# Output blocks copied out by ScalarE and added by GpSimd, with one buffer each for the high half and the e row

## What is computed

```
proj = layernorm(x) @ in_proj_w            # gate 4096, x 4096, B 128, C 128, dt 64
x, B, C = silu(causal_conv4(...))          # per channel
dt = softplus(dt + dt_bias); dA = -dt * exp(A_log); cum = cumsum(dA) per chunk
Y = (C B^T * decay * dt) x  +  C state * exp(cum)  +  D * x      # 64 heads of 64
hidden = Y * silu(gate)
out = (hidden * rsqrt(mean(hidden^2) + eps) * norm_w) @ out_proj_w
```

## Time and profile before

| | us |
|---|---|
| three runs | 1464.09, 1466.99, 1469.27; median 1466.99 |
| profiled execution | 1469.74 |
| its span, first to last instruction | 1468.0 |
| its busy time: PE / DVE / ACT / POOL | 1336.6 / 1190.8 / 1007.1 / 823.1 |

### The profile page before, as it was taken

One profiled execution on the slowest core, in us unless ns is written; L12 is line 12 of the kernel. 1 busy time (PEld: TensorE's weight loads), 2 busy tenths in 40 slices (PEclk: granted clock), 3 DMA queues, 4 the chain that ended last, 5 costly groups with the idle time before them and its releaser, 6 DMA issues. The chain is left out here.

```text
span 1468.0 us, 27111 instructions
## 1 busy us (share of the span) xinstructions
PE 1336.6 (91%) x8896; PEld 1137.1 (77%) x8896; DVE 1190.8 (81%) x2643; ACT 1007.1 (69%) x2067; POOL 823.1 (56%) x896
## 2 busy tenths in 40 slices
PE   5889887767999999999999999999999999986998
PEld 4778776556888888888888888888888888864887
DVE  5753443576999999999999999999999999986433
ACT  1114433667889988888988898888899888861332
POOL 1004211004678787877878787797787878681000
PEclk9999987978999999999999999999999999995999
DMA  6221000223454554454564645644435544324000
GB/s 128 66 87 36 15 15 0 65 65 76 121 111 98 118 125 114 119 112 98 119 125 115 118 101 114 116 123 121 113 101 109 129 113 117 96 73 186 15 14 29
DMA packets 102085, 136.43 MB, mean 93 GB/s; under 512 B 27744, under 2 KB 49856, under 8 KB 101824
## 3 DMA queue, kind: packets, MB, share of 16 engines
q1 hardware_dynamic: 99840, 132.67, 37.6%
q10 hardware_dynamic: 2112, 2.10, 0.4%
HBM read 124.76 MB, written 9.96 MB: 92 GB/s over the span
## 5 line engine op out<-in xcount | busy, mean ns | idle before, releaser
L845 ACT ACTIVATE M<-cum_row,cum_table 128x128 f32<-128x128 f32 x1024 | 312.2, 390 | 0.0
L1240 DVE SCALAR_TENSOR_TENSOR xs<-psum,conv_w_sb,xs 128x509 f32<-128x509 f32 (+2 forms) x384 | 284.2, 740 | 0.4
L985 POOL TENSOR_TENSOR hid_lo<-hid,hid_hi 128x512 fp32r<-128x512 f32 x128 | 191.2, 1494 | 65.4 <-PE psum L40 59.6
L1028 POOL TENSOR_TENSOR hid<-hid,sg 128x512 f32<-128x512 f32 x128 | 165.7, 1295 | 89.5 <-DVE hid L1308 89.4
L1017 POOL TENSOR_TENSOR squares<-squares,sq 128x512 f32<-128x512 f32 x124 | 160.2, 1292 | 75.2 <-ACT sq L822 75.2
L1267 DVE TENSOR_TENSOR M<-M,CB 128x1024 f32<-128x1024 f32 x128 | 182.9, 1429 | 0.0
L1623 PE MATMUL psum<-M,xdt 128*64 128x128 f32 x2048 | 140.1, 279 | 20.8 <-DVE psum L1299 20.8
L827 ACT ACTIVATE sg<-psum 128x512 f32<-128x512 f32 x128 | 75.2, 587 | 102.2 <-PE psum L40 94.6
L1623 PEld LDWEIGHTS psum<-M,xdt 128*64 128x64 f32 x2048 | 109.9, 136 | 43.2 <-DVE M L1267 25.0
L1600 PE MATMUL psum<-xend,B_tok 128*128 128x128 f32 x1024 | 140.3, 281 | 2.1 <-DVE carry L1291 1.9
L859 ACT ACTIVATE xs<-psum,conv_b_sb,conv_w_sb 128x512 f32<-128x512 f32 x128 | 98.7, 771 | 52.7 <-PE psum L40 52.7
(11 more groups left out here) (210 smaller groups left out, 3432.5 us busy)
## 6 DMA issues: line engine op xcount, KB each, us to landing
cum_row<-cum_scratch SPq DMA_DIRECT2D x256, 256.0 KB, 4.6
e_row<-e_scratch SPq DMA_DIRECT2D x256, 128.0 KB, 3.5
xw_raw<-L_attn_in_proj_w_dram SPq DMA_DIRECT2D x32, 128.0 KB, 5.1
wo_raw<-L_attn_out_proj_w_dram SPq DMA_DIRECT2D x32, 128.0 KB, 4.6
gw_raw<-L_attn_in_proj_w_dram SPq DMA_DIRECT2D x16, 256.0 KB, 5.8
x_res<-_attn_hidden_states_dram ACTq DMA_DIRECT2D x4, 512.0 KB, 9.3
x_scratch<-x_res SPq DMA_DIRECT2D x4, 512.0 KB, 2.6
x_res<-x_scratch SPq DMA_DIRECT2D x1, 2048.0 KB, 7.6
```

The source lines that it names most:

```text
L845: last = nc.scalar.activation(M[:, v % 3, h, c * CH:(c + 1) * CH], cum_row[:, v % 2, h, c * CH:(c + 1) * CH], ACT.Relu, bias=scalar_of(CUM ...
L985: nc.gpsimd.tensor_tensor(hid_lo[:], hid[:, v % 2, :], hid_hi[:, v % 2, :].bitcast(F32), ALU.subtract).then_inc(hid_lo_done, 1)
L1028: nc.gpsimd.tensor_tensor(hid[:, v % 2, :], hid[:, v % 2, :], sg[:, v % 8, :], ALU.mult).then_inc(hid_done, 1)
L1240: nc.vector.scalar_tensor_tensor(xs[:, v % 7, shift:], psum[:, X_BANK + v % 2, 0:TT - shift], tap_of(v, step), xs[:, v % 7, shift:], ALU.m ...
```

## The change

`add_out` goes from DVE. In its place ACT, in the slot after a block ends (a phase slot, behind `square`), copies the two PSUM banks out in `take_out`: in the first group straight into `mixed`, later into a new tile `part` with one buffer. POOL then adds the halves of `part` into `mixed` in `add_part`, two and three slots after that phase slot began, that is in the slots with s mod 4 = 2 and 3, behind `gate`, the squares and `split_hid`. `out_proj` of the next block now waits for the copies (`out_taken`), and the copies wait for both adds of the block before (`mixed_done`). `hid_hi` and `e_row` get one buffer each, with their waits one slot nearer. POOL does `gate` ahead of the squares, and in the slots with s mod 4 = 1 the squares come behind `split_hid`. In the phase slots `evac_g` applies silu itself, so one silu of four goes. X_SLOTS and G_SLOTS move ahead by up to a slot.

```diff
-    e_row = sb("e_row", [P, 2, TT], F32)
+    e_row = sb("e_row", [P, TT], F32)
-    hid_hi = sb("hid_hi", [P, 2, TT], F32R)
+    hid_hi = sb("hid_hi", [P, TT], F32R)
+    part = sb("part", [P, KT, TT], F32)
...
-    X_SLOTS = (5, 7, 8, 10)
-    G_SLOTS = (6, 9)
+    X_SLOTS = (5, 7, 7, 9)
+    G_SLOTS = (6, 8)
...
-                sp.wait_ge(off_scaled, nth(v - 2))
+                sp.wait_ge(off_scaled, nth(v - 1))
...
+            def take_out(v):
+
+                t = at_slot(v)[1]
+                act.wait_ge(out_done, nth(v))
+                if v == GP - 1:
+                    act.wait_ge(cum_out, 16 * 2 * NT)
+                if v >= SLOTS:
+                    act.wait_ge(mixed_done, KT * ((v - SLOTS) // GP))
+                for m in range(KT):
+                    to = mixed[:, m, tile(t)] if v < SLOTS else part[:, m, :]
+                    nc.scalar.activation(to, psum[:, OUT_BANK + m, :], ACT.Copy).then_inc(out_taken, 1)
...
             for s in range(-8, ALL):
                 if alive(s):
                     square(s)
+                if s > 0 and s % GP == 0:
+                    take_out(s - 1)
                 phase = s % GP == 0 and alive(s + 4)
                 if phase:
-                    for v in range(s + 4, s + 8):
+                    for v in range(s + 4 if s < 0 else s + 5, s + 8):
                         silu_g(v)
...
-                    evac_g(s + 8)
+                    evac_g(s + 8, ACT.Silu if phase else ACT.Copy)
...
-                pool.wait_ge(out_done, nth(v - 2))
+                pool.wait_ge(out_done, nth(v - 1))
...
+            def add_part(v, m):
+
+                t = at_slot(v)[1]
+                pool.wait_ge(out_taken, KT * (v // GP) + m + 1)
+                nc.gpsimd.tensor_tensor(mixed[:, m, tile(t)], mixed[:, m, tile(t)], part[:, m, :],
+                                        ALU.add).then_inc(mixed_done, 1)
...
             for s in range(-8, ALL):
-                if alive(s):
-                    add_squares(s)
+                after_silu = s % GP == 1
...
                 if alive(s + 1):
                     gate(s + 1)
+                if alive(s) and not after_silu:
+                    add_squares(s)
+                if alive(s + 1):
                     split_hid(s + 1)
+                if alive(s) and after_silu:
+                    add_squares(s)
                 g, u = divmod(s, SLOTS)
+                if s % GP in (2, 3) and SLOTS <= s - s % GP - 1:
+                    add_part(s - s % GP - 1, s % GP - 2)
...
+            for m in range(KT):
+                add_part(ALL - 1, m)
...
-            def add_out(v):
...
-                if s >= 0 and s % GP == GP - 1:
-                    add_out(s)
...
-                    pe.wait_ge(mixed_done, KT * (v // GP))
+                    pe.wait_ge(out_taken, KT * (v // GP))
```

More of the change, by code:

```diff
@@ L467, in macaron @@
     cum_in, xw_in, wo_in = [[sem(f"{n}{i}") for i in range(2)] for n in ("cum_in", "xw_in", "wo_in")]
-    e_in, gw_in = [sem(f"e_in{i}") for i in range(2)], sem("gw_in")
+    e_in, gw_in = sem("e_in"), sem("gw_in")
     halo_in, halo_step, halo_done = sem("halo_in"), sem("halo_step"), sem("halo_done")
-    folded = sem("folded")
+    folded, out_taken = sem("folded"), sem("out_taken")
     wo_hi_done, wo_lo_done, hid_hi_done, hid_lo_done = [sem(n) for n in ("wo_hi_done", "wo_lo_done", "hid_hi_done", "hid_lo_done")]
@@ L618, in load_e @@
                 head = 2 * pair_of(v)
-                sp.wait_ge(off_scaled, nth(v - 2))
+                sp.wait_ge(off_scaled, nth(v - 1))
                 for h in range(2):
-                    sp.dma_start(e_row[h * HP:(h + 1) * HP, v % 2, :],
+                    sp.dma_start(e_row[h * HP:(h + 1) * HP, :],
                                  e_dram[head + h:head + h + 1, tile(at_slot(v)[1])].partition_broadcast(HP)
-                                 .rearrange("p o t -> p (o t)")).then_inc(e_in[v % 2], 16)
+                                 .rearrange("p o t -> p (o t)")).then_inc(e_in, 16)
             for p in range(2):
@@ L822, in square, with evac_g @@
                 nc.scalar.activation(sq[:], hid[:, v % 2, :], ACT.Square).then_inc(sq_done, 1)
-            def evac_g(v):
+            def evac_g(v, how=ACT.Copy):
                 act.wait_ge(g_proj, nth(v))
                 act.wait_ge(hid_done, nth(v - 8))
-                nc.scalar.activation(sg[:, v % 8, :], bank(G_BANK), ACT.Copy).then_inc(g_evac, 1)
+                nc.scalar.activation(sg[:, v % 8, :], bank(G_BANK), how).then_inc(g_evac, 1)
             def silu_g(v):
@@ L909, in _ @@
                     prep(FFN_TICKS + 8 + s)
+            take_out(ALL - 1)
         @block.gpsimd
@@ L978, in split_hid @@
                 pool.wait_ge(hid_done, nth(v))
-                pool.wait_ge(out_done, nth(v - 2))
+                pool.wait_ge(out_done, nth(v - 1))
                 if v == 0:
                     pool.wait_ge(dA_ready, 2)
-                nc.gpsimd.tensor_copy(hid_hi[:, v % 2, :], hid[:, v % 2, :]).then_inc(hid_hi_done, 1)
+                nc.gpsimd.tensor_copy(hid_hi[:], hid[:, v % 2, :]).then_inc(hid_hi_done, 1)
                 pool.wait_ge(hid_hi_done, nth(v))
-                pool.wait_ge(out_done, nth(v - 1))
-                nc.gpsimd.tensor_tensor(hid_lo[:], hid[:, v % 2, :], hid_hi[:, v % 2, :].bitcast(F32),
+                nc.gpsimd.tensor_tensor(hid_lo[:], hid[:, v % 2, :], hid_hi[:].bitcast(F32),
                                         ALU.subtract).then_inc(hid_lo_done, 1)
@@ L1023, in fold_dt @@
                                         ALU.mult).then_inc(folded, 1)
+            def add_part(v, m):
[3 more added lines that the diff above has]
+                                        ALU.add).then_inc(mixed_done, 1)
             def gate(v):
                 pool.wait_ge(v_done, nth(v))
-                pool.wait_ge(sg_done, nth(v))
+                if v % GP == 0 and v >= GP:
+                    pool.wait_ge(g_evac, nth(v))
+                else:
+                    pool.wait_ge(sg_done, nth(v) - max(v // GP, 0))
                 nc.gpsimd.tensor_tensor(hid[:, v % 2, :], hid[:, v % 2, :], sg[:, v % 8, :], ALU.mult).then_inc(hid_done, 1)
@@ L1055, in _ @@
                     continue
-                if u in X_SLOTS:
-                    split_x((g + 1) * GP + X_SLOTS.index(u))
+                for j in range(GP):
+                    if u == X_SLOTS[j]:
+                        split_x((g + 1) * GP + j)
                 if u in G_SLOTS:
@@ L1296, in scale_off @@
                 dve.wait_ge(off_done, nth(v))
-                dve.wait_ge(e_in[v % 2], (v // 2 + 1) * 32)
+                dve.wait_ge(e_in, (v + 1) * 32)
                 cols = slice(CH if at_slot(v)[1] == 0 else 0, TT)
-                nc.vector.tensor_tensor(psum[:, Y_BANK, cols], psum[:, Y_BANK, cols], e_row[:, v % 2, cols],
+                nc.vector.tensor_tensor(psum[:, Y_BANK, cols], psum[:, Y_BANK, cols], e_row[:, cols],
                                         ALU.mult).then_inc(off_scaled, 1)
@@ L1640, in out_proj @@
                     last = split_matmul(nc, psum[:, OUT_BANK + m, :], wo_hi[:, j, cols], wo_lo[:, j, cols],
-                                        hid_hi[:, v % 2, :], hid_lo[:], start=(j == 0), stop=(j == GP - 1))
+                                        hid_hi[:], hid_lo[:], start=(j == 0), stop=(j == GP - 1))
                 last.then_inc(out_done, 1)
```

## The result

The changed kernel takes 1532.45 us (four runs, 1529.50 to 1532.97) against 1467.38 before; the ratio is 1.0442, 95% interval 1.0424 to 1.0461. The profiled execution took 1532.97, its span is 1531.3, 63.3 us more than before.

A forecast was written before the change was run, and what follows sets the result against it. It took PE and DVE, tied in every slot, to bound the kernel before, and a ring through POOL, ACT and DVE after: 1469.74 + 65 - 5 + 3 = 1532.7, about 1530 for the median; own range 1500 to 1558, 8 in 10 1485 to 1560.

The forecast's parts named there:

- ACT's own chain: ACT's unbroken work: 9.25 us from `evac_x(60)` to `evac_x(61)`; two copies 1.05, then 6.22 less 0.55 to the next phase's `evac_x`.
- The ring: ACT, DVE and POOL waiting on each other through `part`: 33.5 us per four slots against 31.28, plus 0.6 on average for splits.
- X: Zero point of the forecast's times within a phase: the end of ACT's `evac_x(60)`; `gate(56)` was due at X + 19.8.
- Per phase +2.7: Each four-slot phase where ACT waits for the second add takes 34.0 us, +2.7; 24 phases give +65.
- The first group and s = 20, -5: Five phases where ACT doesn't wait and DVE's adds are gone: about -1 us each, -5 in all.
- rival (a): The wait for the second add is hidden and PE sets the pace: about 1440 us, the faster side, chance 0.08.
- The end, +3 and one phase: Behind the last matmul, a copy and two POOL adds, queued behind block 123's adds, replace DVE's last add: +3 us.
- The single buffers at 0: Single `e_row`, with `load_e` issued one slot before its reader: costed at 0, upper bound a few times 1 us.
- (b): The ring is shorter and the next path, DVE at about 32 us per four slots, holds: 1472 to 1495 us, chance 0.11.
- (c): The ring and the old losses just cancel: 1463 to 1471 us, chance 0.04.
- (d): POOL falls behind for good or PE's clock drops in added waits: 1555 to 1600 us, chance 0.05 together with (e).
- (e): Silu on PSUM or the copies bring further table loads, two more per phase: 1591 us, chance 0.05 together with (d).

## Why the prediction was right

The forecast was 1530 and the measured time is 1532.45. The mechanism is the one that was named: ACT's wait for the second add, behind `split_hid` in POOL's queue. That the number agrees to 0.2% is partly luck: errors of single terms, of up to 8 us, cancelled. The steps one by one:

- *ACT's own chain.* 9.25 from `evac_x(60)` to `evac_x(61)`: measured 9.25 (769.07 to 778.32). From the start of the copies to `evac_x(60)` the sum of 1.05 and 5.67 gives 6.72: measured 762.29 to 769.07, 6.78.
- *The ring.* 33.5 where no split stands ahead of `gate`, 34.6 to 34.8 behind u = 6 and 14. The four phases of a group, from one `evac_x` of a phase slot to that of the next, measured 33.28 (904.20 - 870.92), 34.52 (803.59 - 769.07), 32.94 and 34.39. So the forecast of the undisturbed ring was 0.2 to 0.6 too long, that of the disturbed one 0.2 to 0.3. POOL's `gate`, forecast at X + 19.8, came at X + 19.35 and 19.66 in the undisturbed phases and at X + 20.95 and 20.82 behind u = 6 and 14. The 0.2 that DVE's slot was given for `masked(56)` was too much: the `masked` of that place waited for POOL in one phase of four only (1.55 us, 1.22 in the others). The mean was 33.78 against 34.0.
- *Per phase +2.7:* measured +58.1 over 23, 2.53, and +59.6 over the 24 of the forecast (v = 25 to 121). The term of 65 is 5 us too large.
- *The first group and s = 20, -5:* measured -4.8. There ACT doesn't wait, and four slots take 30.3 to 30.4 us instead of 30.3 to 32.5, and the sixteen from v = 5 to 21 take 121.6 instead of 125.1: the gain that rival (a) expected everywhere is real where there is no ring. The -2.8 ahead of v = 5 was not in the sum. 1.9 of it lie between v = 1 and 5, which take 47.27 us instead of 49.17, and 49.17 again in the run with four silus, so it is the silu that goes. The other 0.9 are less than the scatter up to v = 1.
- *The end, +3 and one phase:* +12.9 from v = 117 to the end against 2.7 + 3, or +11 against +3 from v = 121 on, so this term was too small. It missed a wait. In the last eight slots there are no projections, a slot of PE shrinks to 5.4 us, and `out_proj` of the next block reaches ACT's copies before they are made:

```profile
1366.13 0.76 PE L38 MATMUL psum<-hid_hi,wo_hi 128*128 128x512 f32 x1 [3.74 <-ACT part L874]
...
1390.92 1.41 PE L1784 MATMUL psum<-ones,squares 128*128 128x1 f32 x6 [5.35 <-PEq L538]
```

  The rows are PE's timeline at the end of the loop. 3.74 us there are the wait on `out_taken`, for which the prediction has no term. Behind this wait the granted clock stood at 0.50, its lower level of 1.2 GHz, for 5 us (1366 to 1371), and an `out_proj` matmul took 0.63 instead of 0.39 to 0.40; the slot lasted 10.6 us on PE, where the same one took 6.3 before. The second row stands 5.35 behind the last matmul where it stood 1.65 behind it before, +3.7 for the copies and adds at the end, for which +3 was set.
- *The single buffers at 0:* the e row is 0; the high half alone is a gain of 5 to 6 us in the kernel before, which the step had not seen. In the changed kernel that wait is part of the ring; what the ring would be with two buffers for `hid_hi`, no run tried.

Too much in the loop (65 against 59.6), too little at the end (3 against 11) and the 2.8 ahead of v = 5 that no term had cancelled: 63 in the sum, 63.3 in the spans.

Of the rivals, (a) was excluded by POOL's order, as it said, and the experiments show what it would take: with the wait for `part` gone and most of that for `sq`, the same split of work takes 1453.31. (b) gave DVE a next path of about 32; no run shows it. The run with the second add ahead of the split came out at 31.84 with the ring still closed, and with the ring open two of four phases took 30.4. (c) is excluded by the measured +65. (d) and (e): in the loop the clock stayed at 1.00 from v = 5 to 121 and fell only behind that, and each phase has two table loads as before.

Whether the add is better off on ACT and POOL stays undecided here: 1453.31 with it there and 1451.90 with it on DVE, both with the new slots and single buffers, lie within 0.2% of each other. The two differ in more than the add, as the first also has one silu less and another order on POOL and ACT.

## What to carry to other kernels

When work is handed from engine to engine and back through one buffer, follow the buffer round: add up everything queued between its release and its next fill on each engine, and compare that ring with the period; an engine with spare time in sum can still be late each time. Place the instruction that frees the buffer ahead of anything that waits for the event that also starts the next fill. In this kernel a second wait of the same kind (`sq`) stood behind the first, so look at the same place again once the first is gone.

## What the runs showed of the hardware

A `masked` that has begun to wait for POOL gets in ahead of the next POOL instruction, even when that follows without a gap. In the changed kernel a `masked` started at 741.20 while POOL's `hid_lo` ran (to 742.06); it took 1.93, to 743.13, and the `squares` add that POOL began at 742.01 took 2.25 instead of 1.26 to 1.30 (timelines of POOL and DVE):

```profile
740.79 1.27 POOL L1000 TENSOR_TENSOR hid_lo<-hid,hid_hi 128x512 fp32r<-128x512 f32 x1
742.01 2.25 POOL L1032 TENSOR_TENSOR squares<-squares,sq 128x512 f32<-128x512 f32 x1
...
741.20 1.93 DVE L1301 TENSOR_TENSOR M<-M,CB 128x1024 f32<-128x1024 f32 x1
```

It is no single case: of the 128 `masked` of that trace 77 took more than 1.3 us, and each of them ended 1.08 to 1.09 us behind the end of the POOL instruction that was running when it started. So here the delay of DVE was bounded by the rest of one POOL instruction, and the delay of POOL by one `masked`. The Trainium skill, SBUF — State Buffer, Who interferes with whom, says that a VectorE instruction with two SBUF inputs contends with a GpSimd instruction that reads SBUF, and that this contention is an exclusive lock; the rows agree, with 1.22 for a `masked` alone and up to 2.32 behind POOL. Which of the two bears it was worth 5 to 6 us in the kernel before, by nothing but a later start of `hid_hi`.
